# The experts' outputs of a decoder layer, scaled and added to the residual by one VectorE instruction that reads PSUM

## What is computed

```
gate = softmax(x @ W_gate + b_gate)
top_g, top_i = top_k(gate, 2)
combine = sum(one_hot(top_i, E) * top_g[..., None], axis=2)
expert_out = einsum('bsd,edf->bsef', x, W_experts) + b_experts
moe_out = einsum('bsef,bse->bsf', expert_out, combine)
x = layernorm(x + attn_out + moe_out)
```

## Time and profile before

| what | us |
|---|---|
| median of three runs | 1332.31 |
| lowest and highest run | 1330.14, 1338.65 |
| the profiled execution, its own time | 1330.05 |
| its span in the profile | 1328.3 |
| busy: TensorE matmuls | 1240.0 |
| busy: VectorE | 904.8 |
| busy: ScalarE | 776.4 |
| busy: GpSimd | 364.9 |

### The profile page before, as it was taken

One profiled execution on the slowest core, in us unless ns is written; L12 is line 12 of the kernel. 1 busy time (PEld: TensorE's weight loads), 2 busy tenths in 40 slices (PEclk: granted clock), 3 DMA queues, 4 the chain that ended last, 5 costly groups with the idle time before them and its releaser, 6 DMA issues.

```text
span 1328.3 us, 19317 instructions
## 1 busy us (share of the span) xinstructions
PE 1240.0 (93%) x6648; PEld 593.1 (45%) x6648; DVE 904.8 (68%) x1809; ACT 776.4 (58%) x1087; POOL 364.9 (27%) x435
## 2 busy tenths in 40 slices
PE   7888989999999999999999999999999999998995
PEld 4433445444444444444444544444444444453442
DVE  5476776567776677767776677767677777767672
ACT  2254556666566655656656665666556566666564
POOL 2310013222521224311423216122252123322162
PEclk9889999999999999999999999999999999999999
DMA  6824134304443323334422243441243333213300
GB/s 233 137 41 69 38 49 65 49 14 68 65 65 49 48 54 46 65 49 64 66 50 50 32 80 49 65 65 27 41 65 49 50 48 45 55 16 49 49 19 16
DMA packets 49840, 74.85 MB, mean 56 GB/s; under 512 B 8520, under 2 KB 20048, under 8 KB 49488
## 3 DMA queue, kind: packets, MB, share of 16 engines
q1 hardware_dynamic: 48496, 72.70, 33.8%
q10 hardware_dynamic: 1248, 0.92, 0.4%
HBM read 18.02 MB, written 4.19 MB: 17 GB/s over the span
## 4 chain that ended last, share of the span: by engine, by line
PE 76%; DVE 10%; issue 5%; ACT 5%; DMA 2%; SPq 1%; POOL 0%; ACTq 0%; DVEq 0%; POOLq 0%
PE ms L412 37%; PE sc L412 14%; PE op L412 14%; PE mx L412 7%; DVE maxes L831 3%; PE ms L491 2%; PE ms L436 2%; DVE k_parts L746 2%; ACT k_parts L617 1%; ACT probs L677 1%; DMA qs<-q_parts 1%; ACT x L695 1%; DMA qs<-shift_r 1%; DVE ks L915 1%; SPq L362 1%
## 5 line engine op out<-in xcount | busy, mean ns | idle before, releaser
L831 DVE TENSOR_REDUCE maxes<-mx 128x1 f32<-128x512 f32 x1024 | 657.9, 684 | 342.2 <-PE mx L412 341.2
L677 ACT ACTIVATE probs<-sc 128x1024 f32<-128x1024 f32 x512 | 524.3, 1024 | 448.6 <-PE sc L412 443.9
L993 POOL TENSOR_TENSOR x<-x,moe 128x256 f32<-128x256 f32 x256 | 187.0, 730 | 630.5 <-ACT moe L670 605.3
L412 PE MATMUL op<-probs,v 128*32 128x512 f32 x2048 | 276.0, 611 | 2.2 <-ACT probs L677 1.1
L412 PE MATMUL sc<-qs,ks 50*128 50x512 f32 x1024 | 258.1, 501 | 10.7 <-ACT probs L677 6.8
L412 PEld LDWEIGHTS sc<-qs,ks 50*128 50x128 f32 x1024 | 95.9, 184 | 322.9 <-ACT probs L677 225.7
L412 PE MATMUL mx<-ks,qs 48*128 48x512 f32 x1024 | 208.5, 403 | 13.7 <-DVE maxes L831 13.4
L670 ACT ACTIVATE moe<-ms,comb 128x256 f32<-128x256 f32 x256 | 106.7, 472 | 18.4 <-PE ms L412 18.4
L412 PEld LDWEIGHTS mx<-ks,qs 48*128 48x128 f32 x1024 | 98.4, 188 | 21.6 <-DVE maxes L831 17.4
L412 PE MATMUL ms<-we_hi,x2T_hi 128*128 128x512 f32 x256 | 94.9, 451 | 6.3 <-DVE lin L765 3.5
L412 PEld LDWEIGHTS op<-probs,v 128*32 128x32 f32 x2048 | 40.4, 108 | 95.6 <-issue 94.2
(11 more groups left out here) (107 smaller groups left out, 1193.9 us busy)
## 6 DMA issues: line engine op xcount, KB each, us to landing
ks<-k_parts SPq DMA_DIRECT2D x192, 128.0 KB, 4.5
qs<-q_parts SPq DMA_DIRECT2D x189, 128.0 KB, 5.6
xT_s<-in_xT SPq DMA_DIRECT2D x8, 512.0 KB, 4.8
x_s<-in_x SPq DMA_DIRECT2D x8, 512.0 KB, 4.4
ctxT_s<-in_ctxT SPq DMA_DIRECT2D x8, 512.0 KB, 3.9
out<-x SPq DMA_DIRECT2D x7, 512.0 KB, 2.9
qs<-shift_r SPq DMA_DIRECT2D x128, 8.0 KB
probs<-in_we SPq DMA_DIRECT2D x1, 1024.0 KB, 7.7
```

Of the source, the lines that this page charges most:

```text
L412: return nc.tensor.matmul(dst, lhsT, rhs, start=first, stop=last, skip_group_check=True)
L677: nc.scalar.activation(probs[:, (2 * s + h) % 3, :, :], sc[:], ACT.Exp).then_inc(exp_out, 1)
L831: nc.vector.tensor_reduce(maxes[:, g % 2, at:at + 1], mx[:, i % 3, :], AX_X, ALU.max).then_inc(max_out, 1)
L993: nc.gpsimd.tensor_tensor(x2[:, n % 2, t, :], x2[:, n % 2, t, :], moe[:, k % 2, j * D:j * D + D], ALU.add).then_inc(acc, 1)
```

## The change

The ring `moe` and the semaphore `moe_out` go, and so do ScalarE's and GpSimd's parts for `moe` and `be` units. VectorE takes a `moe` unit in two `scalar_tensor_tensor` instructions, each of which reads 256 columns from PSUM, multiplies them with the expert's weight, adds the rows of `x2` and writes them back. It takes a `be` unit by one addition of 512 columns. `acc` counts both, and TensorE now waits for `acc` before it uses the bank again. The matrix products, their order and the tables are as before.

```diff
-    for (task, n), k in ENTRY.items():
-        t = mid_at(task, n) if task in ("be0", "be1") else moe_at(n, int(task[3:]))
-        halves["pool"][t + 1].append((task, 1, n))
...
-        moe = sb("moe", [P, 2, 512])
...
             elif task in ("be0", "be1") or task.startswith("moe"):
-                eng.wait_ge(moe_out, 2 * ENTRY[task, n] + 2)
+                eng.wait_ge(acc, 2 * ENTRY[task, n] + 2)
...
-                elif task.startswith("moe"):
-                    k = ENTRY[task, n]
-                    t, pair = int(task[3:]) // (E // 2), int(task[3:]) % (E // 2)
-                    wait_unit(act, task, n)
-                    act.wait_ge(g_step, G_STEPS * (n + 1))
-                    if k >= 2:
-                        act.wait_ge(acc, 2 * (k - 1))
-                    for j in range(2):
-                        e = 2 * pair + j
-                        nc.scalar.activation(moe[:, k % 2, j * D:j * D + D], bank[:, j * D:j * D + D], ACT.Copy,
-                                             scale=comb[:, t, e:e + 1]).then_inc(moe_out, 1)
...
+                elif task in ("be0", "be1"):
+                    k, h = ENTRY[task, n], int(task[2])
+                    wait_unit(dve, task, n)
+                    dve.wait_ge(ln_out[1], TB * (n + 1))
+                    if k >= 1:
+                        dve.wait_ge(acc, 2 * k)
+                    nc.vector.tensor_tensor(x2[:, n % 2, 2 * h:2 * h + 2, :], bank.rearrange("p (n d) -> p n d", n=2),
+                                            x2[:, n % 2, 2 * h:2 * h + 2, :], ALU.add).then_inc(acc, 2)
+                elif task.startswith("moe"):
+                    k = ENTRY[task, n]
+                    t, pair = int(task[3:]) // (E // 2), int(task[3:]) % (E // 2)
+                    wait_unit(dve, task, n)
+                    dve.wait_ge(g_step, G_STEPS * (n + 1))
+                    dve.wait_ge(ln_out[1], TB * (n + 1))
+                    for j in range(2):
+                        e = 2 * pair + j
+                        if k + j >= 1:
+                            dve.wait_ge(acc, 2 * k + j)
+                        nc.vector.scalar_tensor_tensor(out=x2[:, n % 2, t, :], in0=bank[:, j * D:j * D + D],
+                                                       scalar=comb[:, t, e:e + 1], in1=x2[:, n % 2, t, :],
+                                                       op0=ALU.mult, op1=ALU.add).then_inc(acc, 1)
...
                 if n >= 1:
-                    dve.wait_ge(moe_out, 2 * MOE_ENTRIES * n)
+                    dve.wait_ge(acc, 2 * MOE_ENTRIES * n)
...
-                        nc.gpsimd.tensor_tensor(x2[:, n % 2, t, :], x2[:, n % 2, t, :], moe[:, k % 2, j * D:j * D + D],
-                                                ALU.add).then_inc(acc, 1)
```

More of the change, by code:

```diff
@@ L296, in decoder @@
         g_step, g_exp = sem("g_step"), sem("g_exp")
-        moe_out, acc = sem("moe_out"), sem("acc")
+        acc = sem("acc")
         LN_STEPS = (12, 12, 10)
@@ L654, in take_out @@
                     copy(combT, bank[0:E, :]).then_inc(done, 1)
-                elif task in ("be0", "be1"):
-                    k = ENTRY[task, n]
-                    wait_unit(act, task, n)
-                    if k >= 2:
-                        act.wait_ge(acc, 2 * (k - 1))
-                    copy(moe[:, k % 2, :], bank).then_inc(moe_out, 2)
-                elif task.startswith("moe"):
-                    k = ENTRY[task, n]
-                    t, pair = int(task[3:]) // (E // 2), int(task[3:]) % (E // 2)
-                    wait_unit(act, task, n)
-                    act.wait_ge(g_step, G_STEPS * (n + 1))
-                    if k >= 2:
-                        act.wait_ge(acc, 2 * (k - 1))
-                    for j in range(2):
-                        e = 2 * pair + j
-                        nc.scalar.activation(moe[:, k % 2, j * D:j * D + D], bank[:, j * D:j * D + D], ACT.Copy,
-                                             scale=comb[:, t, e:e + 1]).then_inc(moe_out, 1)
             def exps(s, h):
@@ L979, in other @@
                                             ALU.subtract).then_inc(x2_low, 1)
-                elif task in ("be0", "be1"):
-                    k, h = ENTRY[task, n], int(task[2])
-                    pool.wait_ge(moe_out, 2 * k + 2)
-                    if k >= 1:
-                        pool.wait_ge(acc, 2 * k)
-                    nc.gpsimd.tensor_tensor(x2[:, n % 2, 2 * h:2 * h + 2, :], x2[:, n % 2, 2 * h:2 * h + 2, :],
-                                            moe[:, k % 2, :].rearrange("p (n d) -> p n d", n=2), ALU.add).then_inc(acc, 2)
-                else:
-                    k, t = ENTRY[task, n], int(task[3:]) // (E // 2)
-                    for j in range(2):
-                        pool.wait_ge(moe_out, 2 * k + j + 1)
-                        if k + j >= 1:
-                            pool.wait_ge(acc, 2 * k + j)
-                        nc.gpsimd.tensor_tensor(x2[:, n % 2, t, :], x2[:, n % 2, t, :], moe[:, k % 2, j * D:j * D + D],
-                                                ALU.add).then_inc(acc, 1)
             nc.gpsimd.memset(power[:], -0.5).then_inc(fills, 1)
```

## The result

The changed kernel takes 1372.11 us (median of 4 runs, 1366.13 to 1377.35), the kernel before beside it 1331.22 (4 runs, 1327.26 to 1338.65): ratio 1.0296, 95% interval 1.0258 to 1.0335. It is slower by 3%, as forecast. The profiled executions compare closely, since their granted clocks are alike (mean 0.985 after, 0.986 before): 1366.13 us against 1330.05, the span 1363.9 against 1328.3. The span grew by 35.6 us; the sum of the prediction was 36.4.

A forecast was written before the change was run, and what follows sets the result against it. TensorE, busy 93% of 1328.3 us, was taken to bound the kernel. Waits of 36.4 us at 56 places added to the profiled 1330.05 gave 1366.5, with half the 2.3 to the median 1367.5; range 1347 to 1387.

The forecast's parts named there:

- What is removed: ScalarE's scalings, GpSimd's additions: worth 0; at most 0.7 us of TensorE waits and part of 8.5 for the norm, counted 0.
- The fused instruction: VectorE's 128x256 take-out from PSUM: 0.485 us, between 0.42 and 0.55, derived from the 751 ns of the 512-element kind.
- The seven places of a long layer: Layers 1 to 5, units where TensorE waits for VectorE's take-outs: together 4.75 us per layer, five layers 23.8.
- the slot of moe8: Long layers: later maxima make TensorE wait 0.35 to 0.4, then moe8 waits for its bank; 1.5 us in all.
- The three waits behind shifts: k3c0, kc0 and kc1 in long layers: the unit behind a shift waits for its bank, 0.60 us each.
- The ends of the program: Layers 0, 6 and 7, summed separately: 3.8, 4.1 and 4.7 us.
- Rival (d): TensorE's clock falls to the lower level because of the pauses: beyond 1400 us, chance 0.02.
- half of the 2.3 us between profiled execution and median: Added to 1366.5 us, since the profiled execution of the kernel before lay 2.3 below its median; gives 1367.5.
- The readings of the profile that were promised: Profile after: fused line 125 us, VectorE near 1040, ScalarE 660, GpSimd 157, take-out waits some 25 to 35.
- (a): Faster: the take-outs fit and only the relief shows, if a pair ends within 0.42 us behind a shift; 1322, chance 0.03.
- (b): No change within 1%: VectorE's 420 idle us swallow the work; 0 to 13 us, say 1337, chance 0.06.
- (c): VectorE's lateness does not drain between slots; half of the 130 added us on the path, 1395, chance 0.05.

The follow-up runs named there:

- Experiment 1: The changed kernel with expert units of a slot's second half taken out ahead of the next slot's first maxima: 1344.75 us against 1335.56 before, ratio 1.0057.
- experiment 4: The kernel before plus, at 128 places, two dependent VectorE maxima of 128x312 (one SBUF input) with no bank behind them: 1366.95 us, 1351 at clock 0.985.
- experiment 8: The kernel before with the last four instructions of `choose` one half slot later: 1332.01 us, ratio 0.9976.
- experiment 3: The kernel before plus, at 128 places, a dependent fused VectorE pair with two SBUF inputs on its own tile: 1408.98 us, some 1400 at clock 0.985.
- experiment 5: The changed kernel plus, behind each real pair, a fused VectorE pair on an SBUF tile of its own: 1460.44 us, about 1443 at clock 0.985.

## Why the prediction was right

**What is removed.** Nothing, as forecast, but in two steps that can now be told apart. The norm's wait fell by 5.8 us, and the slots of x1's transpose gained only 0.13 us each, since TensorE then waited for moe8's bank instead. The transpose of the earlier trace rows in the changed kernel, and the pair ahead of it:

```profile
722.48 0.99 DVE L810 SCALAR_TENSOR_TENSOR x<-ms,comb,x 128x256 f32<-128x256 f32 x2
...
723.53 0.66 PE L432 MATMUL ms<-w_ident,x 128*128 128x128 f32 x4 [0.63 <-DVE x L810]
```

The slot starts at 720.50, so the transpose starts at S+3.03; the prediction said S+3.05 where it had been S+3.4. Experiment 1 shows the same gain at full size, 0.72.

**The fused instruction.** 480 ns, forecast 485, bounds 420 and 550. The pair is 0.99 us from its first start to its second end, as 0.485 + 0.04 + 0.485 would give. The page "VectorE: DVE Perf Modes" of the Trainium skill, in its section on the TRN2 errata, gives (N + 151)/0.96 ns for a plain fp32 addition, by which one of 256 elements would take 424, an estimate; carried over to the fused kind it would be too short by 56 ns (480 measured). The choice to go by the row of 751 ns for 512 was the right one: that a surcharge read at one width carries over to another was an assumption, and it held.

**The seven places of a long layer.** Named right, and sized within 0.08 us each but for one. The term that was too large is the slot of moe8, 1.5 where 1.29 was measured (1.28 in the layer shown: 714.66 to 720.50, before 699.86 to 704.42):

```profile
716.24 1.26 DVE L831 TENSOR_REDUCE maxes<-mx 128x1 f32<-128x512 f32 x2
...
716.95 0.50 PE L408 MATMUL mx<-ks,qs 48*128 48x512 f32 x2
...
717.41 1.00 DVE L810 SCALAR_TENSOR_TENSOR x<-ms,comb,x 128x256 f32<-128x256 f32 x2
...
718.46 0.74 PE L408 MATMUL ms<-we_hi,x2T_hi 128*128 128x512 f32 x2 [0.79 <-DVE x L810]
```

Both links are there: the maxima's matmuls come 0.53 us behind the scores of 716.42 where they came 0.34 behind in the kernel before (701.53, and 701.87 in the earlier trace rows), and moe8 waits for moe7's bank. But with S = 714.66 this pair of maxima starts at S+1.58, where the forecast had 701.53 - 699.86 = S+1.67, and moe8 at S+3.80 in place of S+3.94. The step took the pair to be late by the full length of the fused one; in the kernel before it had itself waited some 0.1 us for TensorE's matmuls of 700.20 (the aggregation could be followed from 700.52), which the lateness used up first. The three waits behind shifts were 0.06 to 0.08 too small each. kc1 starts 0.03 us earlier than forecast, but takes longer: its row is 1.98 us where it was 1.88, since its first weights too are loaded only when the bank is free. A wait for a bank costs this 0.1 us on top, which the prediction didn't count.

**The ends of the program.** These were worked out more coarsely, and the errors partly cancel: layer 0 was 0.85 us too small, layer 7 too large by 1.4. Of that, 0.6 is a gain in two of its last slots, those of moe13 and moe14, which the sum had at 0; what makes it was not looked into. Layer 6 was right, 4.1 and 4.0, with the gain at x2T0, 0.75 forecast and 0.72 measured. Without the clock's 1.3 us the slots give 35.0, so the sum by places was 4% too large. That 36.4 is also what the slots with the clock give, and that the span's 35.6 is so near, is luck: it takes the clock's 1.3, the shorter start and the longer end to get there.

**The clock.** The step that was missing. Rival (d) thought of a clock that stays low and was given 0.02; what happens is smaller and more common, falls of 3 to 10 us, in both kernels and mostly at the same places of the program (the slots of gate, moe0 and moe1 around the choice, in layer 0 also moe10, and some at both ends), in some executions more and in some fewer. The prediction counted half of the 2.3 us between profiled execution and median, and it was 6.0 for the change, whose four executions had clocks of 0.985, 0.984, 0.980 and 0.975 and took 1366.13, 1368.81, 1375.41 and 1377.35 us. At clock 0.985, near that of the profiled execution from which the forecast counts (0.986), the change takes 1368.5 where 1367.5 was forecast.

**The readings of the profile that were promised.** The fused line (125 us, measured 123.0), GpSimd (157, 158.2) and the waits for take-outs (25 to 35, 27.5, none over 0.8) came out. VectorE was put at 1040 and shows 1014.9: the new instructions' own durations come to 134 (256 x 0.48 and 16 x 0.68), but the busy time grew by 110, since it counts once what overlaps, and each pair starts and ends some 0.08 us inside its neighbours, by my estimate 20 of the 24. ScalarE shows 681 where 660 was forecast, for the same reason the other way round. The wait for maxima was to grow by 2 to 5 us and did not (13.4, 13.3); the lateness stands in the weights' row and in the slot's length. The single wait of over 1 us in the slot of moe8 is two, 0.79 and a part ahead of the maxima.

**The rivals.** (a), faster, falls with the pair's 0.99 us against the 0.42 it allowed. (b) falls with 51 waits. (c), lateness that does not drain, did not come about: slots with moe13 and moe14 did not grow. But lateness that costs something within its own slot is real: experiment 4 shows it at 16 to 19 us. In the change it is part of the cost at moe8, as the prediction had it, and behind shifts it is covered by the wait for the bank.

**Open.** What makes the clock fall at these places, and whether a kernel could avoid it, was not settled: the pause ahead of moe0 stands in five long layers of the kernel before in which the clock of the profiled execution did not fall, and experiment 8 only divides it. Whether moving the shift's copy off VectorE would free the rest of experiment 1's loss was not tried.

## What to carry to other kernels

Ask not how busy the engine is that takes the new work, but where in its fixed order the new work stands and who needs the buffer that it frees: here 74% busy and 36 us lost, of which three quarters went by putting the same instructions ahead of a pair of reductions. A sum by places, so many slots times the lateness of one end, was good to 4% here, with errors of up to 1.4 us in single layers, and it needs only a slot's timeline, a duration from a near row and the program's order. And look at the granted clock of every execution before two times are compared: 0.01 of it was worth 8.5 us here, more than most of the edits.

## What the runs showed of the hardware

- A VectorE instruction of 128x256 with both inputs in SBUF takes 472 to 485 ns alone, and had a mean of 825 and a longest of 1404 beside GpSimd's additions and norms (experiment 3, whose median over all is 837); with the additions gone the median was 484 (experiment 5). GpSimd's additions went from 730 to 757 on the mean: the two engines do not share the loss evenly.
- The same instruction with one input in PSUM took 473 to 486 in all 256 cases (the change), also in the 38 that overlap what GpSimd still does there, and a reduction with one SBUF input had a median of 477 and a longest of 480 beside GpSimd's additions (experiment 4).
- The granted clock falls for 3 to 10 us at a time, mostly at the same places of the program, at a cost of some 1.1 us for each of the short ones, and how many of these places are hit differs from one execution to the next of the same kernel: 1327.36 to 1342.48 us with nothing changed.
